# P times V in bursts of eight: batch size and copy position in an attention stage on one core

## The chip, the cores and the metric

The kernel runs on one core of a Trainium2 chip, in one launch. The metric is the device time of that launch in microseconds, the median over runs. A core has TensorE (PE; its weight loads are shown as PEld), VectorE (DVE), ScalarE (ACT), GpSimd (POOL) and SyncE (SP), which run their own instruction streams and meet only at semaphores.

## What is computed

```python
x = x + 0.5 * ffn(layernorm(x))        # x: 2048 x 128, float32
x = x + attention(layernorm(x))        # 16 heads of 8, rotary q and k, softmax over 2048 keys
x = x + 0.5 * ffn(layernorm(x))

# in attention, for each head:
scores = q @ k.T / sqrt(8)
attn = softmax(scores)
out = attn @ v
return concat(out) @ wo.T + bo

# ffn: ternary weights (128 -> 512 -> 128), exact gelu, layernorm between them
```

## The kernel before, in words

The program has three stages: the first feed-forward part with the projections, attention, and the second feed-forward part. The change lies in attention alone. There the 16 heads are 8 pairs, and the queries 4 chunks of 512. One unit `w` is one pair against one chunk: 32 of them. For a unit, TensorE, ScalarE and VectorE each walk through their own list of steps.

TensorE's list is `steps` (L1116). Step `k` of the 32 (`B_STEP`) of a unit is 128 keys of one head of the pair against 512 queries:

- `exp_mm` (L1074, matmul L1084) makes the scores, transposed, in one of three PSUM banks (`EXP`). It waits for `p_ready`, so that the exponential three steps back has left the bank. The scores already have the row's maximum subtracted: it stands in three rows of the operand `QS`.
- `max_mm` (L1058, matmul L1069) makes half of a 128 x 1024 block of scores for a later unit (23 blocks ahead), from which VectorE takes a maximum per query (L689). Two slots of two PSUM banks each hold these blocks (`A0`, a slot freed by `a_free`). The two matmuls of a step use different halves of the array's rows.
- After every fourth step (`BATCH = 4`), `pv_batch` (L1087, matmul L1095) multiplies the four exponentials of the batch before with V. They are float32, and each of the four goes to its own 32 columns of the array and 32 partitions of one PSUM bank (`PO`): two heads, even and odd key tiles. The sums grow in `PO` over the unit.
- After step 23 (`SPLIT - 1`) comes `shared` (L1099): the maxima of the next unit are transposed, and the finished sums of the unit before are turned and added by four small matmuls (L1112).
- In the last pass, `late` (L1134) slips transposes and the output projection of the finished chunks in behind some steps (`LATE`, L81).

ScalarE's list is `exps` (L897): `exp_unit` (L883, L887) turns a bank of scores into a slot of `ring`, which has 16 slots of 128 x 512 float32; every `BATCH` of them it waits (L886) until the batch that used these slots has been multiplied. After exponential `OUT_AT` (4) of a unit, `take_out` (L890, L895) copies the finished sums of the unit before from `PO` to `outT`; the first `pv_batch` of the unit waits for that copy (`po_free`, L1090).

The order of TensorE's work is thus written out by hand: a burst of P times V stands between the matmuls of one step and those of the next, and all of them are executed in order. SyncE and GpSimd only load query operands and rows of maxima, one unit or more ahead. The first three of the four chunks are a hardware loop (`Fori`), the last one is straight code, and its last units have no `max_mm` left.

A float32 matmul leaves two records in the trace: L1095 has 2048 records for 1024 multiplications, and the burst of four is x8.

Of the kernel before, what the change touches and what calls it, by code (L numbers as in the profile page):

```python
# [42 lines left out]

A_STEP = 2 * CT * 2
B_STEP = 2 * NT
BATCH = 4
NB = B_STEP // BATCH
LEAD = 23
PRING = 16
# [3 lines left out]
SHARED_AT = 12  # L53
SPLIT = 2 * SHARED_AT
TOP_AT = 2 * A_STEP - LEAD
OUT_AT = 4

A_IT = PAIRS * A_STEP
B_IT = PAIRS * B_STEP
# [9 lines left out]
def shared_slot(w, last=False):  # L69

    units = LEAD + A_STEP * w + SHARED_AT
    return (min(units, A_IT) if last else units) + w + 1
# [8 lines left out]
LATE = {(6, 5): ("T", 0), (6, 6): ("O", 0), (6, 7): ("T", 1), (7, 0): ("O", 1), (7, 1): ("F", 0),  # L81
        (7, 2): ("T", 2), (7, 3): ("O", 2), (7, 5): ("F", 1), (7, 7): ("F", 2)}
# [13 lines left out]
C_ONE = 1  # L96
C_RING = PRING // BATCH

# [11 lines left out]
def macaron(nc, x, wq, bq, wk, bk, wv, bv, wo, bo, w_fc, ln_w, ln_b, w_proj, out):  # L110
    rope_dram = nc.inline_tensor(rope_tables(), name="rope_tables").ap()

    with ExitStack() as ctx:
        def sb(name, shape, dt=F32):
            return ctx.enter_context(nc.sbuf_tensor(name, shape, dt))
# [22 lines left out]
        ring = sb("ring", [P, PRING, CS])  # L138
# [121 lines left out]
        def late_banks(c):  # L260

            return (PR[1] + 1, PR[1]) if c == NC - 1 else (A0 + 1, A0 + 3)
# [547 lines left out]
        def _(act):  # L810
# [72 lines left out]
            def exp_unit(k, c):  # L883
                act.wait_ge(b_ready, c * B_IT + k + 1)
                if k % BATCH == 0:
                    act.wait_ge(pv_done, c * PV_IT + k // BATCH + 1)  # L886
                a.activation(ring[:, k % PRING, :], ps[:, EXP[k % C_EXP], :], ACT.Exp, scale=SCALE)\  # L887
                    .then_inc(p_ready, 1)

            def take_out(i, c):  # L890

                act.wait_ge(pv_done, c * PV_IT + (i + 1) * NB + C_RING)

                act.wait_ge(a_ready, c * SLOT_IT + shared_slot(i - 1, type(c) is int) + 1)
                a.copy(outT[:, i % 2, :], ps[:, PO, :]).then_inc(po_free, 1)  # L895

            def exps(w, start, stop, c):  # L897
                for k in range(start, stop):
                    exp_unit(w * B_STEP + k, c)
                    if k == OUT_AT and (w or type(c) is not int):  # L900
                        take_out(w - 1, c)
# [16 lines left out]
        def _(pe):  # L918
# [30 lines left out]
            for n in range(2):  # L949
                for k in range(KH):  # L950
                    last = t.transpose(psb[:, TR[n], k * P:(k + 1) * P], tern[:, n, k * P:(k + 1) * P], identb[:, :])
# [106 lines left out]
            def max_mm(m, c):  # L1058

                n, x = m // 2, m % 2  # L1060
                i, u, s = n // A_STEP, n % A_STEP, unit_slot(n)
                j = i % PAIRS
                h, q, half = u % 2, u // 2 % CT, u // (2 * CT)
                if x == 0:
                    if u == 0:
                        pe.wait_ge(q_in[j], (c + i // PAIRS + 1) * 16)
                    slot_free(s, c)
                rows = slice(HR * h, HR * h + R_QK)
                mm = t.matmul(ps[:, A0 + 2 * (s % 2) + x, :], QS[rows, j, q * P:(q + 1) * P],  # L1069
                              KT[rows, j, (2 * half + x) * 512:(2 * half + x + 1) * 512], start=True, stop=True)  # L1070
                if x:
                    mm.then_inc(a_ready, 1)

            def exp_mm(i, k, c):  # L1074

                b, r4 = k // BATCH, k % BATCH
                h, kt = r4 // 2, 2 * b + r4 % 2
                n, j = i * B_STEP + k, i % PAIRS
                if k == 0:
                    pe.wait_ge(m_in[j], (c + i // PAIRS + 1) * 32)  # L1080

                pe.wait_ge(p_ready, c * B_IT + n + (C_EXP if n == SPLIT else 1))
                rows = slice(HR * h, HR * h + R_ALL)
                t.matmul(ps[:, EXP[n % C_EXP], :], KT[rows, j, kt * P:(kt + 1) * P], QS[rows, j, :],  # L1084
                         start=True, stop=True).then_inc(b_ready, 1)

            def pv_batch(i, b, c):  # L1087

                if b == 0:
                    pe.wait_ge(po_free, c * PAIRS + i + C_ONE)  # L1090
                pe.wait_ge(p_ready, c * B_IT + i * B_STEP + (b + 1) * BATCH + C_EXP)
                for r4 in range(BATCH):
                    h, kt = r4 // 2, 2 * b + r4 % 2
                    col = (2 * (i % PAIRS) + h) * VW
                    mm = t.matmul(ps[32 * r4:32 * r4 + 32, PO, :], Vx[:, kt, col:col + 32],  # L1095
                                  ring[:, (b * BATCH + r4) % PRING, :], start=(b == 0), stop=(b == NB - 1))
                mm.then_inc(pv_done, 1)

            def shared(w, c, last=False):  # L1099


                s = shared_slot(w, last)
                if not last or w < PAIRS - 1:
                    pe.wait_ge(mp_ready, c * PAIRS + w + 2)
                slot_free(s, c)
                if not last or w < PAIRS - 1:
                    mm = t.transpose(psb[0:2 * 3 * CT, A0 + 2 * (s % 2) + 1, 0:P], mp[:, (w + 1) % 2, :],
                                     identb[:, :])
                if type(c) is not int or w > 0 or last:
                    pe.wait_ge(po_free, c * PAIRS + w + C_ONE)  # L1110
                    for q in range(CT):
                        mm = t.matmul(ps[:, A0 + 2 * (s % 2), q * 2 * VW:(q + 1) * 2 * VW],  # L1112
                                      outT[:, (w - 1) % 2, q * P:(q + 1) * P], pick[:, :], start=True, stop=True)
                mm.then_inc(a_ready, 1)

            def steps(w, start, stop, c, last=False):  # L1116

                for k in range(start, stop):
                    exp_mm(w, k, c)
                    m = w * B_STEP + k + 2 * LEAD  # L1120
                    if not last or m < 2 * A_IT:
                        max_mm(m, c)
                    if k % BATCH == BATCH - 1:
                        b = k // BATCH
                        if b:
                            pv_batch(w, b - 1, c)
                        elif w or type(c) is not int:
                            pv_batch(w - 1, NB - 1, c)
                    if k == SPLIT - 1:
                        shared(w, c, last)  # L1130
                    if last and k % BATCH == BATCH - 1 and (w, k // BATCH) in LATE:
                        late(*LATE[w, k // BATCH])

            def late(kind, c):  # L1134

                if kind == "O":
                    pe.wait_ge(taken, TURNED["T", c] + 1)
                    pe.wait_ge(x1_ready, c + NC + C_TWO)
                    for i in range(CT):
                        last = t.matmul(ps[:, late_banks(c)[1], i * D:(i + 1) * D], XOT[:, i * P:(i + 1) * P],  # L1140
                                        WT[:, 3, :], start=True, stop=True)
                    last.then_inc(o_ready, 1)
                    return
                if kind == "T":
                    pe.wait_ge(xo_ready, c + 1)
                else:
                    pe.wait_ge(xn_ready, c + 2 * NC + 1)
                if TURNED[kind, c]:
                    pe.wait_ge(taken, TURNED[kind, c])
                else:  # L1150

                    pe.wait_ge(a_free, (NC - 1) * SLOT_IT + shared_slot(PAIRS - 2, True) + 1)
                for i in range(CT):
                    last = t.transpose(ps[:, late_banks(c)[0], i * P:(i + 1) * P], (XO if kind == "T" else xn)[:, i, :],
                                       ident[:, :])
                last.then_inc(turned, 1)
# [10 lines left out]
            for m in range(2 * (TURNS - 2), 2 * LEAD):  # L1167
# [5 lines left out]
                if m == 2 * (LEAD - A_STEP) + SPLIT - 1:  # L1173
                    shared(-1, 0)
            pe.wait_ge(xt_ready, 2 * NC + C_ONE)
            steps(0, 0, SPLIT, 0)
            with pe.Fori(0, NC - 1) as c:
                steps(0, SPLIT, B_STEP, c)
                for w in range(1, PAIRS):
                    steps(w, 0, B_STEP, c)  # L1180
                steps(PAIRS, 0, SPLIT, c)
            steps(0, SPLIT, B_STEP, NC - 1, True)
            for w in range(1, PAIRS):
                steps(w, 0, B_STEP, NC - 1, True)
            pv_batch(PAIRS - 1, NB - 1, NC - 1)
            shared(PAIRS, NC - 1, True)

# [42 lines left out]
```

## Time and profile before

| | |
|---|---|
| median of 3 runs | 894.6 us (891.29 to 894.69) |
| the profiled execution | 889.24 us |
| its span, first to last instruction | 887.4 us |
| mean granted TensorE clock | 0.953 of full speed |
| attention stage, first exponential to the last P times V | 151.6 to about 836.5 us |
| exponentials (L887) | 1024, mean 605 ns |
| maxima (L689) | 512, mean 1219 ns |

A row of a timeline has the start in us, the length in us from the first start to the last end, the engine, the line and operation, what it writes and reads with shapes, how many instructions are merged in it, and in brackets the idle time of the engine before them with what released it. Instructions of one engine can overlap, so several in one row are shorter than their sum. A row of windows has, for each engine, busy time and instructions, and PEclk, the granted clock as a share of full speed.

### The profile page before, as it was taken

How to read it: one execution, taken by the hardware profiler on the slowest of the kernel's cores; microseconds unless marked ns; L12 is line 12 of the kernel's file. 1: busy time of each engine (PE TensorE's matmuls, PEld its weight loads, DVE VectorE, ACT ScalarE, POOL GpSimd, SP SyncE). 2: the span in 40 equal slices, each digit the busy share in tenths (PEclk: the TensorE clock that was granted, in tenths of full speed). 3: DMA queues.
4: the chain of work that ended last, by engine and by line, in shares of the span. 5: the costliest groups of instructions: out<-in, count | busy, mean ns of one | idle time of the engine just before them, and what ended most of it. 6: DMA issues, size and time to landing. Idle time of an engine off the chain costs nothing.

```text
span 887.4 us, 16511 instructions
## 1 busy us (share of the span) xinstructions
PE 794.1 (89%) x5207; PEld 271.5 (31%) x5207; DVE 772.9 (87%) x1043; ACT 606.2 (68%) x1144; POOL 112.1 (13%) x273
## 2 busy tenths in 40 slices
PE   5876679999999998999999899999999999998885
PEld 3654431222222222222222222222222222223364
DVE  6889988899999997999999889999999999984376
ACT  2214751788888886888778778888888888884611
POOL 3344330000000000001000000000000000001023
PEclk9997885999999998999999999999999999998999
DMA  4000010000000000000000000000000000000001
GB/s 101 1 1 0 0 48 1 7 7 8 8 7 8 8 8 9 8 7 7 8 7 7 10 8 7 7 8 13 8 8 1 1 2 1 2 1 1 1 12 36
DMA packets 8239, 8.72 MB, mean 10 GB/s; under 512 B 2784, under 2 KB 6496, under 8 KB 8160
## 3 DMA queue, kind: packets, MB, share of 16 engines
q0 software_dynamic: 1536, 4.20, 1.3%
q1 hardware_dynamic: 4272, 2.82, 1.1%
q10 hardware_dynamic: 2352, 0.66, 0.4%
q8 instruction: 48, 0.79, 0.4%
q14 instruction: 31, 0.25, 0.1%
HBM read 2.23 MB, written 1.05 MB: 4 GB/s over the span
## 4 chain that ended last, share of the span: by engine, by line
PE 57%; ACT 17%; issue 13%; DVE 8%; POOL 3%; ACTq 1%; DVEq 0%; DMA 0%; POOLq 0%; SPq 0%
PE ps L1095 25%; PE ps L1084 21%; ACT ring L887 15%; PE ps L1069 4%; PE ps L1112 4%; ACT outT L895 2%; DVE mh L689 2%; POOL XB L341 1%; PE ps L942 1%; DVE xn L461 1%; DVE X L647 1%; DVE terms L642 1%; DVE ring L637 1%; PE ps L1140 1%; ACTq L886 1%
## 5 line engine op out<-in xcount | busy, mean ns | idle before, releaser
L887 ACT ACTIVATE ring<-ps 128x512 f32<-128x512 f32 x1024 | 532.6, 605 | 163.8 <-PE ps L1084 162.1
L689 DVE TENSOR_REDUCE mh<-ps 128x1 f32<-128x1024 f32 x512 | 603.1, 1219 | 38.0 <-PE ps L1069 25.3
L1069 PE MATMUL ps<-KT,QS 48*128 48x512 bf16 x1024 | 354.7, 396 | 3.4 <-DVE mh L689 2.5
L1084 PE MATMUL ps<-QS,KT 51*128 51x512 bf16 x1024 | 314.9, 390 | 33.0 <-ACT ring L887 20.6
L1095 PE MATMUL ps<-ring,Vx 128*32 128x512 f32 x2048 | 276.7, 613 | 2.6
L1084 PEld LDWEIGHTS ps<-QS,KT 51*128 51x128 bf16 x1024 | 76.1, 94 | 334.3 <-ACT ring L887 294.3
L1069 PEld LDWEIGHTS ps<-KT,QS 48*128 48x128 bf16 x1024 | 75.6, 94 | 84.0 <-DVE mh L689 60.1
L409 POOL TENSOR_TENSOR mp<-zeros,top 128x8 bf16<-128x8 f32 x32 | 6.2, 194 | 470.1 <-DVE top L699 470.1
L1095 PEld LDWEIGHTS ps<-ring,Vx 128*32 128x32 f32 x2048 | 40.6, 108 | 64.6 <-issue 49.9
L829 ACT ACTIVATE ring<-ps 128x512 f32<-128x512 f32 x32 | 17.2, 602 | 45.7 <-DVE ring L524 25.3
L418 POOL DMA_DIRECT2D QS<-QT x32 | 18.1, 567 | 154.3 <-PE ps L1084 154.3
L1038 PE MATMUL ps<-identb,terms 128*128 128x128 bf16 x256 | 22.9, 256 | 14.0 <-ACT QT L874 8.7
L1112 PE MATMUL ps<-pick,outT 128*128 128x18 f32 x256 | 34.1, 267 | 0.8 <-ACT outT L895 0.8
L990 PE MATMUL ps<-WpC,ring 128*128 128x129 f32 x256 | 31.3, 281 | 3.2 <-ACT ring L829 2.4
L1112 PEld LDWEIGHTS ps<-pick,outT 128*128 128x128 f32 x256 | 31.0, 191 | 10.1 <-issue 10.1
L990 PEld LDWEIGHTS ps<-WpC,ring 128*128 128x128 f32 x256 | 30.8, 197 | 5.5 <-issue 3.0
L931 PE MATMUL ps<-QT,WfcT 128*128 128x512 f32 x64 | 29.5, 601 | 0.8 <-ACT QT L825 0.7
L519 DVE TENSOR_TENSOR ring<-ring 128x512 f32<-128x512 f32 x32 | 22.7, 714 | 7.7 <-ACT ring L829 7.7
L1038 PEld LDWEIGHTS ps<-identb,terms 128*128 128x128 bf16 x256 | 18.6, 115 | 20.6 <-ACT QT L874 11.2
L708 DVE COPY mrow<-ps 24x128 bf16<-24x128 bf16 x32 | 6.8, 211 | 20.3 <-PE ps L1112 20.3
L524 DVE TENSOR_TENSOR ring<-ring 128x512 f32<-128x512 f32 x24 | 21.2, 884 | 1.8
L461 DVE TENSOR_SCALAR xn<-X,mv,rs 128x128 f32<-128x128 f32 (+1 forms) x48 | 21.4, 532 | 0.9 <-PE ps L926 0.5
(110 smaller groups left out, 385.9 us busy)
## 6 DMA issues: line engine op xcount, KB each, us to landing
QS<-QT POOLq DMA_DIRECT2D x32, 128.0 KB, 2.0
QS<-mrow SPq DMA_DIRECT2D x64, 3.0 KB
out_dram<-X SPq DMA_DIRECT2D x4, 256.0 KB, 2.3
wfc_n<-in_L_ffn_W_fc_dram SPq DMA_DIRECT2D x1, 256.0 KB, 3.1
wpj_n<-in_L_ffn_W_proj_dram SPq DMA_DIRECT2D x1, 256.0 KB, 3.6
rope<-rope_tables ACTq DMA_DIRECT2D x1, 128.0 KB, 6.2
w_n<-in_L_attn_wq_dram ACTq DMA_DIRECT2D x1, 64.0 KB, 3.4
w_n<-in_L_attn_wk_dram ACTq DMA_DIRECT2D x1, 64.0 KB, 6.6
```

Source lines behind the costliest of these rows:

```text
L461: last = v.tensor_scalar(xn[:, i, :], rows_of(src, c, i), mv[:, b * CT + i, 0:1], rs[:, b * CT + i:b * CT + i + 1], ALU.subtract, ALU.mult)
L519: v.tensor_tensor(sq[:, k, :], hid[:, k, :], hid[:, k, :], ALU.mult)
L524: return v.tensor_tensor(sqsum[:, k - 1, :], sqsum[:, k - 2, :] if k > 1 else sq[:, 0, :], sq[:, k, :], ALU.add)
L689: v.tensor_reduce(mh[:, n // A_STEP % 2, at:at + 1], ps[:, slot_banks(s), :].rearrange("p a b -> p (a b)"), AX.X, ALU.max).then_inc(a_free, 1)
L887: a.activation(ring[:, k % PRING, :], ps[:, EXP[k % C_EXP], :], ACT.Exp, scale=SCALE)\
L931: t.matmul(ps[:, FC + k, :], WfcT[:, k * P:(k + 1) * P], XF[:, bass.ds(c * CS, CS)], start=True, stop=True).then_inc(fc_ready, 1)
L990: last = t.matmul(out_tile(i, parity)[:, 0:D + 1], hid[:, k, i * P:(i + 1) * P], WpC[:, k, :], start=(k == 0), stop=(k == KH - 1))
L1038: last = t.transpose(psb[:, TR[m % 3], (j * CT + i) * P:(j * CT + i + 1) * P], terms[:, n, i, 4 * e + 2 * j:4 * e + 2 * j + 2, :] .rearran ...
L1069: mm = t.matmul(ps[:, A0 + 2 * (s % 2) + x, :], QS[rows, j, q * P:(q + 1) * P], KT[rows, j, (2 * half + x) * 512:(2 * half + x + 1) * 512] ...
L1084: t.matmul(ps[:, EXP[n % C_EXP], :], KT[rows, j, kt * P:(kt + 1) * P], QS[rows, j, :], start=True, stop=True).then_inc(b_ready, 1)
L1095: mm = t.matmul(ps[32 * r4:32 * r4 + 32, PO, :], Vx[:, kt, col:col + 32], ring[:, (b * BATCH + r4) % PRING, :], start=(b == 0), stop=(b == ...
L1112: mm = t.matmul(ps[:, A0 + 2 * (s % 2), q * 2 * VW:(q + 1) * 2 * VW], outT[:, (w - 1) % 2, q * P:(q + 1) * P], pick[:, :], start=True, sto ...
```

## The change

The batch is eight exponentials: `NB` falls from 8 to 4 batches per unit, `C_RING` (`PRING // BATCH`, L97) from 4 to 2, so the ring of 16 holds two batches. `pv_batch` runs after every eighth step, and multiplies the eight exponentials of the batch before in one go; a new constant `GROUP = 4` keeps the mapping of a step to head, key tile and 32-column group as it was. ScalarE waits for the ring once in eight. `OUT_AT` goes from 4 to 8: the copy of the finished sums stands behind exponential 8 of the next unit. The late work of the last pass keeps its steps.

```diff
--- before.py
+++ after.py
@@ -43,7 +43,8 @@
 
 A_STEP = 2 * CT * 2
 B_STEP = 2 * NT
-BATCH = 4
+GROUP = 4
+BATCH = 8
 NB = B_STEP // BATCH
 LEAD = 23
 PRING = 16
@@ -53,7 +54,7 @@
 SHARED_AT = 12
 SPLIT = 2 * SHARED_AT
 TOP_AT = 2 * A_STEP - LEAD
-OUT_AT = 4
+OUT_AT = 8
 
 A_IT = PAIRS * A_STEP
 B_IT = PAIRS * B_STEP
@@ -1073,8 +1074,8 @@
 
             def exp_mm(i, k, c):
 
-                b, r4 = k // BATCH, k % BATCH
-                h, kt = r4 // 2, 2 * b + r4 % 2
+                r4 = k % GROUP
+                h, kt = r4 // 2, 2 * (k // GROUP) + r4 % 2
                 n, j = i * B_STEP + k, i % PAIRS
                 if k == 0:
                     pe.wait_ge(m_in[j], (c + i // PAIRS + 1) * 32)
@@ -1089,11 +1090,12 @@
                 if b == 0:
                     pe.wait_ge(po_free, c * PAIRS + i + C_ONE)
                 pe.wait_ge(p_ready, c * B_IT + i * B_STEP + (b + 1) * BATCH + C_EXP)
-                for r4 in range(BATCH):
-                    h, kt = r4 // 2, 2 * b + r4 % 2
+                for k in range(b * BATCH, (b + 1) * BATCH):
+                    r4 = k % GROUP
+                    h, kt = r4 // 2, 2 * (k // GROUP) + r4 % 2
                     col = (2 * (i % PAIRS) + h) * VW
                     mm = t.matmul(ps[32 * r4:32 * r4 + 32, PO, :], Vx[:, kt, col:col + 32],
-                                  ring[:, (b * BATCH + r4) % PRING, :], start=(b == 0), stop=(b == NB - 1))
+                                  ring[:, k % PRING, :], start=(k < GROUP), stop=(k >= B_STEP - GROUP))
                 mm.then_inc(pv_done, 1)
 
             def shared(w, c, last=False):
@@ -1128,8 +1130,8 @@
                             pv_batch(w - 1, NB - 1, c)
                     if k == SPLIT - 1:
                         shared(w, c, last)
-                    if last and k % BATCH == BATCH - 1 and (w, k // BATCH) in LATE:
-                        late(*LATE[w, k // BATCH])
+                    if last and k % GROUP == GROUP - 1 and (w, k // GROUP) in LATE:
+                        late(*LATE[w, k // GROUP])
 
             def late(kind, c):
```

## Rows read from the trace of the kernel before

**Rows 1.** The page: busy time by engine, the exponentials, and the chain by engine.

```profile
PE 794.1 (89%) x5207; PEld 271.5 (31%) x5207; DVE 772.9 (87%) x1043; ACT 606.2 (68%) x1144; POOL 112.1 (13%) x273
...
L887 ACT ACTIVATE ring<-ps 128x512 f32<-128x512 f32 x1024 | 532.6, 605 | 163.8 <-PE ps L1084 162.1
...
PE 57%; ACT 17%; issue 13%; DVE 8%; POOL 3%; ACTq 1%; DVEq 0%; DMA 0%; POOLq 0%; SPq 0%
```

**Rows 2.** Windows: busy time of each engine, granted clock (PEclk), by stretch.

```profile
23.00:71.00 48.00, 36.97 (x209) 27.36 (x210) 42.01 (x107) 8.54 (x16) 21.06 (x21) 0.93 0.00 1
...
172.00:332.00 160.00, 152.07 (x1053) 41.26 (x1045) 148.92 (x153) 130.71 (x255) 11.46 (x43) 1.00 0.03 8
```

**Rows 3.** Timeline of ScalarE, loop code.

```profile
301.52 0.58 ACT L895 COPY outT<-ps 128x512 f32<-128x512 f32 x1
...
308.52 2.06 ACT L887 ACTIVATE ring<-ps 128x512 f32<-128x512 f32 x4 [0.41 <-PE ps L1084]
...
310.99 2.06 ACT L887 ACTIVATE ring<-ps 128x512 f32<-128x512 f32 x4 [0.41 <-PE ps L1084]
...
314.50 2.06 ACT L887 ACTIVATE ring<-ps 128x512 f32<-128x512 f32 x4 [1.44 <-PE ps L1084]
...
322.41 0.58 ACT L895 COPY outT<-ps 128x512 f32<-128x512 f32 x1
...
322.87 3.73 ACT L887 ACTIVATE ring<-ps 128x512 f32<-128x512 f32 x7
```

**Rows 4.** Timeline of TensorE, one period of the loop.

```profile
309.18 0.39 PE L1084 MATMUL ps<-QS,KT 51*128 51x512 bf16 x1
...
309.50 1.06 PE L1095 MATMUL ps<-ring,Vx 128*32 128x512 f32 x8
...
310.49 0.39 PE L1084 MATMUL ps<-QS,KT 51*128 51x512 bf16 x1
...
310.94 0.38 PE L1084 MATMUL ps<-QS,KT 51*128 51x512 bf16 x1
...
311.11 0.39 PE L1069 MATMUL ps<-KT,QS 48*128 48x512 bf16 x1
...
311.65 0.39 PE L1084 MATMUL ps<-QS,KT 51*128 51x512 bf16 x1 [0.15 <-ACT ring L887]
```

**Rows 5.** Timelines of TensorE: first and second round of a burst; dense float32 matmuls.

```profile
302.16 0.64 PE L1095 MATMUL ps<-ring,Vx 128*32 128x512 f32 x4
...
302.61 0.61 PE L1095 MATMUL ps<-ring,Vx 128*32 128x512 f32 x4
...
840.46 1.88 PE L931 MATMUL ps<-QT,WfcT 128*128 128x512 f32 x4
```

**Rows 6.** Timeline of VectorE, loop code.

```profile
303.83 7.22 DVE L689 TENSOR_REDUCE mh<-ps 128x1 f32<-128x1024 f32 x6 [0.27 <-PE ps L1069]
...
314.71 9.73 DVE L689 TENSOR_REDUCE mh<-ps 128x1 f32<-128x1024 f32 x8
```

**Rows 7.** Timeline of ScalarE, last pass (between two copies: one unit).

```profile
706.21 0.58 ACT L895 COPY outT<-ps 128x512 f32<-128x512 f32 x1
...
726.55 0.58 ACT L895 COPY outT<-ps 128x512 f32<-128x512 f32 x1
```

**Rows 8.** Timeline of ScalarE where no maxima are left.

```profile
817.82 2.06 ACT L887 ACTIVATE ring<-ps 128x512 f32<-128x512 f32 x4 [0.58 <-PE ps L1084]
...
820.79 2.06 ACT L887 ACTIVATE ring<-ps 128x512 f32<-128x512 f32 x4 [0.91 <-PE ps L1084]
...
824.27 2.06 ACT L887 ACTIVATE ring<-ps 128x512 f32<-128x512 f32 x4 [1.41 <-PE ps L1084]
...
826.66 2.06 ACT L887 ACTIVATE ring<-ps 128x512 f32<-128x512 f32 x4 [0.33 <-PE ps L1084]
```

**Rows 9.** Timeline of ScalarE behind the stall between two passes.

```profile
338.10 2.06 ACT L887 ACTIVATE ring<-ps 128x512 f32<-128x512 f32 x4 [4.15 <-PE ps L1084]
...
341.89 2.06 ACT L887 ACTIVATE ring<-ps 128x512 f32<-128x512 f32 x4 [1.73 <-PE ps L1084]
```

## The prediction

> **What bounds the kernel now.** I read the page first: TensorE, VectorE and ScalarE are all busy for most of the span, and the chain that ended last runs over TensorE for 57% and ScalarE for 17% [rows 1]. So no single engine's busy time is the answer. The windows show the same through the attention stage (from 151.64 to 836 us; 1024 exponentials): in 160 us TensorE is busy for 152.07, VectorE for 148.92, ScalarE for 130.71, at full clock [rows 2]. Everything that the change touches lies in this stage, and it repeats, so I read it as a rhythm.
>
> The rhythm on ScalarE: four exponentials in 2.06 us, then an idle stretch of 0.41 us that ends with the matmul at L1084; starts at 308.52 and 310.99, so four exponentials per 2.47 us [rows 3]. Four alone would take less: (2.06 - 0.605)/3 = 0.485 us from start to start (0.605 us is the mean of one [rows 1]), 1.94 us for four. ScalarE is held up once in four, always at the exponential behind a burst of P times V. One period is a closed loop [rows 4, 5]: the score matmul of the last step of a four starts at 309.18, when a PSUM bank of the three comes free; the burst starts 0.32 later (309.50) and takes 0.99 until the next score matmul can start (310.49); its exponential starts 0.50 later (310.99) and takes 0.61; its end frees the bank for the next such score matmul, 0.05 later (311.65). Sum 0.32 + 0.99 + 0.50 + 0.61 + 0.05 = 2.47. The other three exponentials run beside the burst.
>
> Does VectorE set this period too? Its maxima follow each other every (9.73 - 1.22)/7 = 1.22 us at most, (7.22 - 1.22)/5 = 1.20 at best, so it needs 2.40 to 2.43 of each 2.47 us [rows 6]: close, not above. The decisive rows come from the end of the stage, in the last pass, where no maxima are left: the period is 826.66 - 824.27 = 2.39 us [rows 8]. Earlier in that pass, with all the maxima, a unit of 32 exponentials lasts 726.55 - 706.21 = 20.34 us [rows 7]; taking 1.04 us for its shared step (below), 19.3 are left for eight periods: 2.41. So maxima or none, the period is the same (the pass is straight code; that it is 0.08 shorter than in the loop I put down to wait arithmetic on ScalarE). The loop of TensorE and ScalarE sets the time, and the burst is on it. An extra batch of transposes behind a burst gave 820.79 - 817.82 = 2.97, which is 2.39 plus its own length [rows 8]. In [rows 3] the shared transposes and four small matmuls give 314.50 - 310.99 = 3.51, 1.04 more than 2.47. What is put behind a burst is paid in full.
>
> In the loop a unit lasts 322.41 - 301.52 = 20.89 us (between two copies of finished sums): 8 x 2.47 + 1.04 = 20.80, so the copy itself costs 0.09 [rows 3]. There are 32 units, 24 of them by loop code.
>
> **The change, step by step.** Take eight exponentials as the new period and count from the start of the score matmul of step 7 of the eight, which waits as before for the fourth exponential back to free its bank.
> 1. The burst. It starts at 0.32 as now. In a burst of four, each multiplication leaves two records; the four run side by side, and the second round starts 302.61 - 302.16 = 0.45 us behind the first [rows 5]. Two rounds are 0.90, the whole takes 0.99. I take 0.90 for the added four: 1.89 in all. Bounds: 0.99 each if nothing is shared between the fours; 2 x (1.88 - 0.60)/3 = 0.85 if the second four runs as densely as the records of L931 do [rows 5]. The score matmul of step 8 starts at 0.32 + 1.89 = 2.21, its exponential 0.50 later at 2.71. The exponential that freed the bank began 0.05 + 0.61 before zero, so the third behind it ends at 3 x 0.485 + 0.605 - 0.66 = 1.40, and ScalarE idles 1.31 us, where it idled 0.41 (by the same count 1.81 - 1.40).
> The 0.09 that is left over in today's burst, and 0.32 - 0.22 = 0.10 before it (score matmuls otherwise follow each other at (310.94 - 310.49)/2 = 0.22 [rows 4]), look like a price of going in and out of the 32-column form. The Trainium skill, TensorEngine Tiling, section Key Properties, says that a change of tiling mode, unlike a change of tile, drains TensorE. The trace agrees in that both ends of a burst have such gaps. By that rule the added four costs 0.90, without it 0.99, which is 128 x 0.09 = 12 us more.
> 2. The half without a burst. Exponentials 8 to 12 then follow without a hole: 12 starts at 2.71 + 4 x 0.485 = 4.65, ends at 5.26, and the next score matmul of a step 7 starts at 5.31. Against 2 x 2.47 = 4.94 now. So the second half gives back 2.47 - 1.94 = 0.53, and the burst takes 0.90: 0.37 net.
> 3. VectorE. TensorE starts no maxima for 2.2 us. The first unit of scores after the burst is ready at 2.21 + 0.22 + 0.39 + 0.05 = 2.87; VectorE, which needs 4.8 us per eight, has by then run dry and starts it at once; two maxima later, at 2.87 + 1.20 + 1.22 = 5.29, the slot is free that the block of step 14 needs, and the score matmul of step 15 is queued behind it: 5.35 instead of 5.31. Today both slots hold work for VectorE during a burst (8 maxima without a hole [rows 6]); this cover is gone. I take 5.35 (in the last pass the ScalarE way gives 5.23, and VectorE's 5.35 decides). Bounds: nothing, if the wait doesn't fall in with the score matmul, to 0.2 more per period, about one stall as it stands at L1069 now (its matmul starts at 311.11, its partner at 310.94 [rows 4]).
> 4. The copy of the sums, later. Now it lies behind exponential 4, in the hole before 8: of its 0.46 us (322.87 - 322.41 [rows 3]), 0.09 show. After the change it stands behind exponential 8, and there is no hole until 12, which frees the bank on which the next period hangs. ScalarE's way becomes 5.31 + 0.46 = 5.77 in that period: 0.42 over 5.35, 0.33 more than its price now. Bounds 0 and 0.46. Its readers are far: TensorE wants the bank at step 15, the shared matmuls at step 23.
> 5. The shared step sits at step 23, behind a burst now and then: 1.04 in both. Semaphores: half as many batch increments and waits, on no path that I find; the ring wait of exponential 8 is for the burst that its own score matmul is behind anyhow. No DMA is moved; the queues of SyncE and GpSimd lead by many steps.
> 6. The end: the last batch waits for the last exponential and is eight: +0.9 us by step 1. Two or three of the late transposes of the last pass now fall outside a burst, where TensorE has time: -2 us.
>
> Sum. A unit in the loop: 4 x 5.35 + 1.04 + 0.42 = 22.86, minus 20.89 = 1.97; 24 units: 47 us. The last pass: 22.86 - 20.34 = 2.52; 8 units: 20 us. The end: -1. Together +66 us. The profiled execution took 889.24 us (span 887.4), so 955; the median of the runs is 894.6, 5.4 above it, and my number is for the median: 894.6 + 66 = **960 us**.
>
> **Rivals.**
> a) VectorE holds TensorE harder: each maximum after the burst waits, and the score matmul queued behind it too, so the losses of ScalarE and VectorE add up. For: VectorE has hardly more than 0.04 to 0.07 of 2.47 us to spare. Against: with the longer period it gets 0.5 us. Price 0.25 more per eight, 128 x 0.25 = 32: 992 us. Chance 0.10.
> b) The clock falls. TensorE is granted full clock (2.4 GHz) through the stage, except behind stalls such as the one of 4.15 us on ScalarE before 338.10; behind it, at half clock (1.2 GHz) at first, the period of four is 341.89 - 338.10 = 3.79 us, 1.32 more [rows 9]. The change lowers TensorE's work per time by some 7%. Against: from 23 to 71 us the granted clock was 0.93 with TensorE busy 36.97 of 48 us, though no less a share than I expect here [rows 2]. If the stage were granted that 0.93, 0.14 of the periods would be at half clock, each longer by those 1.32 and another 0.9 for the added four: 128 x 0.14 x 2.2 = 40 us: 1000 us. Chance 0.05.
> c) VectorE is the real bound, and TensorE's absence hides behind its two slots: 895 us, no change. For: it is busy 149 of 160 us. Against: the period without maxima is the same [rows 7, 8]. Chance 0.04.
> d) Faster: TensorE is the bound (busy 152 of 160 us), and half of the entries and exits of bursts are saved, 128 x (0.10 + 0.09) = 24 us: 871 us. It decides only if the burst never leaves ScalarE dry, that is if a burst is shorter than the exponentials that stand ready behind it: 0.32 + 1.89 + 0.50 must be under the 1.40 of step 1, and even today's 1.81 is not. This is what the rule of TensorEngine Tiling in the Trainium skill would give if it stood alone. Chance 0.03.
> That the change doesn't do what it says: the eight stand in one loop without a wait between them, so no split is possible; I give it 0.01, at 895 us.
>
> **How the numbers follow.** The forecast has 0.77, a) 0.10, b) 0.05, c) 0.04, d) 0.03, no effect 0.01. Bounds of the terms: burst -6 to +12 us, VectorE -8 to +26, copy -13 to +2. All at their ends give 66 - 27 = 39 and 66 + 40 = 106: 934 to 1001; for the spread of the runs (891.29 to 894.69) two more below. The range 932 to 1000 holds the forecast and a), and just reaches b); c), d) and no effect stay out with 0.08. A measurement of this kernel can tell about 0.5% (4.5 us) from no change. Faster: 0.03; same: 0.05; slower: 0.92.
>
> **What would show it.** In the profile after: ScalarE's row x8, or two rows with one hole in eight of about 1.3 us before it, released by L1084; eight exponentials per 5.35 us; sixteen records of L1095 in about 1.95 us, the next score matmul 1.89 behind the first; a unit of about 22.9 us; a VectorE that waits about 0.5 us per eight for L1069. Step 1 is wrong if the burst is not 1.85 to 2.0; step 3 if the period differs from 5.35 with a burst of 1.89; step 4 if the period with the copy is no 0.4 longer than the others. The prediction as a whole is wrong if ScalarE's hole stays at 0.4, or if the granted clock leaves 1.0 in the steady stretches.

## The result, and the profile after

The changed kernel takes 1095.9 us (median of 4 runs, 1088.8 to 1098.6) against 892.9 us for the kernel before beside it (4 runs, 890.4 to 894.7): 1.226 times as long, 95% interval 1.219 to 1.233. The direction was forecast, the size was not: 960 us was predicted, with 932 to 1000 as the range. The runs of a kernel spread, by 2% in one case below, and every ratio here goes by those within 1.5% of the fastest.

The page of the profile after: the span, busy times, the line of granted clock by slice, and the three engines' main groups.

```profile
span 1096.8 us, 16358 instructions
...
PE 965.2 (88%) x5206; PEld 311.5 (28%) x5207; DVE 767.9 (70%) x1043; ACT 594.5 (54%) x1144; POOL 112.1 (10%) x273
...
PEclk9978657888897878788978887889788987887899
...
L690 DVE TENSOR_REDUCE mh<-ps 128x1 f32<-128x1024 f32 x512 | 599.9, 1218 | 182.9 <-PE ps L1070 181.7
...
L888 ACT ACTIVATE ring<-ps 128x512 f32<-128x512 f32 x1024 | 520.4, 629 | 379.9 <-PE ps L1085 379.5
...
L1097 PE MATMUL ps<-ring,Vx 128*32 128x512 f32 x2048 | 356.1, 831 | 0.0
```

Two of these lines as the page before has them:

```profile
PEclk9997885999999998999999999999999999998999
...
L1095 PE MATMUL ps<-ring,Vx 128*32 128x512 f32 x2048 | 276.7, 613 | 2.6
```

The work is the same, the instructions nearly so [rows 1]: VectorE's maxima have the same mean, 1218 ns against 1219. But P times V now has 831 ns per record where the page before had 613, and the PEclk line, which stood at 9 in the middle but for one slice of 8, is mostly at 7 and 8 through the attention stage, with single slices of 9. ScalarE idles 379.9 us in front of its exponentials, 163.8 before.

Windows of the changed kernel in the attention stage (columns as in [rows 2]; the third number from the end is the granted clock). The first stretch lies in the first pass of the loop in every kernel here:

```profile
172.00:332.00 160.00, 145.56 (x801) 39.02 (x805) 113.61 (x118) 98.05 (x196) 9.36 (x36) 0.83 0.02 6
...
355.00:500.00 145.00, 131.95 (x713) 35.22 (x709) 99.87 (x104) 86.65 (x173) 7.79 (x30) 0.81 0.02 6
```

Granted clock 0.83 and 0.81; the kernel before has 1.00 in both stretches. The first timeline is ScalarE's. A row x8 is one period; the number in brackets is the hole behind a burst.

```profile
405.99 4.03 ACT L888 ACTIVATE ring<-ps 128x512 f32<-128x512 f32 x8 [3.80 <-PE ps L1085]
...
413.28 0.60 ACT L888 ACTIVATE ring<-ps 128x512 f32<-128x512 f32 x1 [3.26 <-PE ps L1085]
...
413.77 0.58 ACT L896 COPY outT<-ps 128x512 f32<-128x512 f32 x1
...
414.24 3.56 ACT L888 ACTIVATE ring<-ps 128x512 f32<-128x512 f32 x7
...
420.64 4.03 ACT L888 ACTIVATE ring<-ps 128x512 f32<-128x512 f32 x8 [2.85 <-PE ps L1085]
...
427.15 4.03 ACT L888 ACTIVATE ring<-ps 128x512 f32<-128x512 f32 x8 [2.48 <-PE ps L1085]
...
434.32 4.03 ACT L888 ACTIVATE ring<-ps 128x512 f32<-128x512 f32 x8 [3.14 <-PE ps L1085]
...
439.79 0.60 ACT L888 ACTIVATE ring<-ps 128x512 f32<-128x512 f32 x1 [1.45 <-PE ps L1085]
```

There are two kinds of period, those at full clock (2.4 GHz) and those that are partly at half clock (1.2 GHz). From 434.32 to 439.79 one lasts 5.47 us: that is the schedule at full clock, 0.12 over the forecast 5.35. From 405.99 to 413.28 one lasts 7.29, and its hole is 3.26 us instead of 1.45. (From 427.15 to 434.32 are 7.17 us.) TensorE's timeline shows the difference, first a burst at half clock, then one at full clock with the thin half of the period ahead of it. Between them stands the end of another thin half and its burst:

```profile
409.27 3.48 PE L1097 MATMUL ps<-ring,Vx 128*32 128x512 f32 x16
...
412.69 0.47 PE L1085 MATMUL ps<-QS,KT 51*128 51x512 bf16 x1
...
415.89 0.39 PE L1085 MATMUL ps<-QS,KT 51*128 51x512 bf16 x1
...
416.38 0.61 PE L1085 MATMUL ps<-QS,KT 51*128 51x512 bf16 x1
...
416.92 3.29 PE L1097 MATMUL ps<-ring,Vx 128*32 128x512 f32 x16
...
420.14 0.39 PE L1085 MATMUL ps<-QS,KT 51*128 51x512 bf16 x1
...
433.81 0.39 PE L1085 MATMUL ps<-QS,KT 51*128 51x512 bf16 x1
...
436.90 0.39 PE L1070 MATMUL ps<-KT,QS 48*128 48x512 bf16 x1
...
436.99 0.38 PE L1085 MATMUL ps<-QS,KT 51*128 51x512 bf16 x1
...
437.13 0.38 PE L1070 MATMUL ps<-KT,QS 48*128 48x512 bf16 x1
...
437.43 1.92 PE L1097 MATMUL ps<-ring,Vx 128*32 128x512 f32 x16
...
439.29 0.39 PE L1085 MATMUL ps<-QS,KT 51*128 51x512 bf16 x1
```

At full clock the next score matmul starts 1.86 us behind the start of the burst, at half clock 3.42. Between bursts, over 3.6 us (433.81 to 437.43), TensorE has eight pairs of score matmuls, which follow each other 0.22 us apart where nothing holds them, and otherwise it waits. The rows show where the clock changes: a score matmul takes 0.39 at 415.89 and 0.61 at 416.38, the last one before the burst, the burst behind it takes 3.29, and the score matmul at 420.14 takes 0.39 again. So here the clock falls at the end of a thin half, and is back after the burst. Through the stage the falls show in the second half of such a stretch or in the burst behind it, the ends of a pass aside. In TensorE's timeline from 170 us on, 60 of 123 bursts take over 2.7 us and 63 under 2 us.

Of the 203 us, how much is schedule and how much is clock? That is what the experiments are about. The ratio of each is to the kernel before, run on the same chip.

### The profile page after: what moved, and what is told of

Same layout as the page of the kernel before. It is cut to its first block, busy times and chain, and to the rows that moved or that the text cites. A ratio compares the mean times of both kernels' runs of the same rounds, so it can differ in the third digit from the quotient of the medians.

```text
span 1096.8 us, 16358 instructions
## 1 busy us (share of the span) xinstructions
PE 965.2 (88%) x5206; PEld 311.5 (28%) x5207; DVE 767.9 (70%) x1043; ACT 594.5 (54%) x1144; POOL 112.1 (10%) x273
## 3 DMA queue, kind: packets, MB, share of 16 engines
q1 hardware_dynamic: 4272, 2.82, 0.9%
## 4 chain that ended last, share of the span: by engine, by line
PE 59%; DVE 16%; issue 13%; ACT 9%; DVEq 1%; POOL 1%; ACTq 0%; DMA 0%; POOLq 0%; SPq 0%
PE ps L1097 32%; PE ps L1085 11%; DVE mh L690 10%; PE ps L1070 9%; ACT ring L888 7%; PE ps L1114 3%; ACT outT L896 2%; PE ps L932 1%; DVE xn L462 1%; DVEq L524 1%; PE ps L943 1%; POOL XB L342 1%; PE ps L1027 1%; DVE X L648 0%; DVE terms L643 0%
## 5 line engine op out<-in xcount | busy, mean ns | idle before, releaser
L690 DVE TENSOR_REDUCE mh<-ps 128x1 f32<-128x1024 f32 x512 | 599.9, 1218 | 182.9 <-PE ps L1070 181.7
L888 ACT ACTIVATE ring<-ps 128x512 f32<-128x512 f32 x1024 | 520.4, 629 | 379.9 <-PE ps L1085 379.5
L1085 PE MATMUL ps<-QS,KT 51*128 51x512 bf16 x1024 | 381.6, 423 | 60.8 <-ACT ring L888 43.3
L1070 PE MATMUL ps<-KT,QS 48*128 48x512 bf16 x1024 | 368.0, 435 | 18.1 <-DVE mh L690 11.7
L1097 PE MATMUL ps<-ring,Vx 128*32 128x512 f32 x2048 | 356.1, 831 | 0.0
L1085 PEld LDWEIGHTS ps<-QS,KT 51*128 51x128 bf16 x1024 | 88.0, 96 | 341.7 <-ACT ring L888 241.6
L1097 PEld LDWEIGHTS ps<-ring,Vx 128*32 128x32 f32 x2048 | 65.8, 134 | 180.1 <-issue 133.3
L1070 PEld LDWEIGHTS ps<-KT,QS 48*128 48x128 bf16 x1024 | 84.7, 97 | 111.1 <-DVE mh L690 74.5
L830 ACT ACTIVATE ring<-ps 128x512 f32<-128x512 f32 x32 | 17.2, 602 | 44.3 <-DVE ring L525 25.5
L1027 PE MATMUL ps<-WT,ring 128*128 128x384 f32 x32 | 19.0, 765 | 5.5 <-ACT ring L826 5.5
```

The source lines that it names most:

```text
L690: v.tensor_reduce(mh[:, n // A_STEP % 2, at:at + 1], ps[:, slot_banks(s), :].rearrange("p a b -> p (a b)"), AX.X, ALU.max).then_inc(a_free, 1)
L1027: t.matmul(ps[:, FC + i, 0:3 * D], XT[:, i * P:(i + 1) * P], WT[:, 0:3, :].rearrange("p n d -> p (n d)"), start=True, stop=True).then_inc( ...
```

## The experiments

**Bursts of four in the changed kernel.** The eight of a batch are multiplied as four behind step 3 and four behind step 7. All else of the change stays: the ring wait once in eight, one semaphore step per batch, the copy behind exponential 8.

```diff
...
-                    if k % BATCH == BATCH - 1:
-                        b = k // BATCH
+                    if k % GROUP == GROUP - 1:
+                        b, half = k // BATCH, k % BATCH // GROUP
                         if b:
-                            pv_batch(w, b - 1, c)
+                            pv_batch(w, b - 1, c, half)
...
```

> The changed kernel, but the eight of a batch are multiplied as four behind step 3 and four behind step 7; ring wait once in eight and the copy behind exponential 8 stay. If the burst length alone makes the loss (stall behind a burst of 1.86 us, and the lower granted clock that comes with it): 890 to 900 us, granted clock about 0.95, eight exponentials per 4.94 us as before. If the coarser ring wait or the later copy carries a good part of the loss: over 920 us.

Measured: 888.9 us, ratio 0.995 (0.993 to 0.998), granted clock 0.942. ScalarE's timeline:

```profile
405.12 2.07 ACT L888 ACTIVATE ring<-ps 128x512 f32<-128x512 f32 x4 [1.44 <-PE ps L1085]
...
407.51 2.06 ACT L888 ACTIVATE ring<-ps 128x512 f32<-128x512 f32 x4 [0.33 <-PE ps L1085]
...
409.98 2.06 ACT L888 ACTIVATE ring<-ps 128x512 f32<-128x512 f32 x4 [0.41 <-PE ps L1085]
...
412.38 2.06 ACT L888 ACTIVATE ring<-ps 128x512 f32<-128x512 f32 x4 [0.33 <-PE ps L1085]
```

The whole loss is gone, so it hangs on the length of the burst (and of the thin half that comes with it), and not on the coarser waits or the later copy by themselves. The result is even 0.5% faster than the kernel before: in the loop the periods of four alternate between 2.39 (405.12 to 407.51) and 2.47 us (407.51 to 409.98), where the kernel before had 2.47 throughout [rows 3]. That fits the ring wait, which now stands ahead of every second four only: in these rows the four after a hole of 0.41 us (409.98) has it, the ones after 0.33 don't. No run moves this wait by itself. It is the fastest version of this study.

**A fuller thin half.** The score matmul is issued twice in steps 2 to 6 of each eight, into the same bank with the same values. The burst, and all waits, stay as in the changed kernel.

```diff
+DOUBLED = (2, 3, 4, 5, 6)
...
-                t.matmul(ps[:, EXP[n % C_EXP], :], KT[rows, j, kt * P:(kt + 1) * P], QS[rows, j, :],
-                         start=True, stop=True).then_inc(b_ready, 1)
+                for _ in range(1 + (k % BATCH in DOUBLED)):
+                    mm = t.matmul(ps[:, EXP[n % C_EXP], :], KT[rows, j, kt * P:(kt + 1) * P], QS[rows, j, :],
+                                  start=True, stop=True)
+                mm.then_inc(b_ready, 1)
```

> The changed kernel with the score matmul issued twice in steps 2 to 6 of each eight (same values into the same bank), so that TensorE works in the half without a burst too: more work, same burst. Theory (the clock is granted by how evenly TensorE is busy, and half of the loss or more is the clock): clock over 0.93 and 945 to 975 us, faster than the changed kernel by 12%. Rival (the clock falls because of the long burst of 32-column matmuls itself, or the loss is all schedule): clock stays near 0.82, time 1095 to 1140 us.

Measured: 978.4 us, ratio 1.094 (1.086 to 1.102), granted clock 0.939. TensorE does more, and the kernel is 117 us faster than the changed one. First a window, then ScalarE's timeline:

```profile
172.00:332.00 160.00, 154.66 (x1076) 46.34 (x1080) 132.29 (x138) 114.83 (x230) 10.94 (x42) 1.00 0.02 7
```

```profile
404.40 0.58 ACT L897 COPY outT<-ps 128x512 f32<-128x512 f32 x1
...
409.69 4.03 ACT L889 ACTIVATE ring<-ps 128x512 f32<-128x512 f32 x8 [1.26 <-PE ps L1087]
...
416.22 4.03 ACT L889 ACTIVATE ring<-ps 128x512 f32<-128x512 f32 x8 [2.50 <-PE ps L1087]
...
421.73 4.03 ACT L889 ACTIVATE ring<-ps 128x512 f32<-128x512 f32 x8 [1.48 <-PE ps L1087]
...
427.22 0.60 ACT L889 ACTIVATE ring<-ps 128x512 f32<-128x512 f32 x1 [1.47 <-PE ps L1087]
...
427.72 0.58 ACT L897 COPY outT<-ps 128x512 f32<-128x512 f32 x1
```

The clock is 1.00 (in 355 to 500 us it is 0.96; of that, 360 to 380 us, with the stall between two passes of the loop, has 0.74, and every other 20 us have 1.00), and the periods are those that the changed kernel had at full clock: 427.22 - 421.73 = 5.49 us, 5.51 between 416.22 and 421.73, hole 1.48. So at most 978.4 - 893 = 85 us are the schedule's, and some 117 are the clock's (1095.9 - 978.4). The units agree: one lasts 427.72 - 404.40 = 23.32 us in the loop against 20.89 before, and 804.03 - 780.87 = 23.16 in the last pass against 20.34, 24 x 2.43 + 8 x 2.82 = 81 us. The burst is as long as in the changed kernel, so it isn't the long burst as such that lowers the clock: 4 of 127 bursts take over 2.7 us.

**Three added matmuls, in two places.** The same edit with `DOUBLED = (3, 4, 5)`, the middle of the thin half, and with `DOUBLED = (7, 0, 1)`, on both sides of the burst.

> As e2_fill, but only three score matmuls in eight are issued twice, in the middle of the thin half (steps 3, 4, 5). Theory (the clock falls because TensorE's work is thin for 3.6 us at a time): the middle of the thin half is what counts, clock over 0.90, time 960 to 1000 us. Rival (a threshold of total work): the same clock as e6_near3, whatever it is.

> The same three added matmuls per eight, put next to the burst (steps 7, 0, 1), where TensorE is dense anyway; the thin half stays as thin as in the changed kernel. Theory: clock stays under 0.87, time over 1070 us (two of the three also lengthen the hole, 0.44 us per eight). Rival (total work): the same clock as e5_fill3.

Measured: 992.8 us (ratio 1.111, 1.104 to 1.117) in the middle, and 1159.1 us (1.299, 1.294 to 1.305) beside the burst. The windows, first of the one in the middle, then of the one beside the burst:

```profile
172.00:332.00 160.00, 147.53 (x999) 42.82 (x999) 129.24 (x135) 111.55 (x223) 10.93 (x42) 0.98 0.02 7
...
355.00:500.00 145.00, 132.62 (x877) 38.76 (x878) 112.81 (x119) 97.86 (x195) 9.35 (x36) 0.95 0.02 7
```

```profile
172.00:332.00 160.00, 144.88 (x829) 41.09 (x833) 108.61 (x113) 95.99 (x188) 9.43 (x36) 0.86 0.02 6
...
355.00:500.00 145.00, 130.35 (x739) 37.37 (x733) 95.04 (x100) 84.24 (x163) 7.66 (x30) 0.84 0.02 6
```

The same added work keeps the clock at 0.98 and 0.95 in one place and leaves it at 0.86 and 0.84 in the other; 13 of 127 bursts take over 2.7 us in the one, 54 of 116 in the other. The second window of both holds a stall between two passes, so the first is the better to compare. The sum of the work per eight exponentials doesn't decide, its place does. (Beside the burst the matmuls also lengthen the period, to 424.59 - 418.60 = 5.99 us at full clock, 0.51 more: 128 x 0.51 = 65 us, and this kernel is 63 us slower than the changed one at a slightly higher clock.) That it is the thinnest stretch that decides is the reading that fits, not a thing these runs separate from others.

**Bursts of four at the pace of the changed kernel.** To the kernel before, two small copies on ScalarE are added in each four exponentials, so that its period is as long as half of the changed kernel's, while TensorE's work stays evenly spread.

```diff
...
+                if k % BATCH == 1:
+                    act.wait_ge(spared, c * PV_IT + k // BATCH)
+                    a.copy(spare[:, 0:H], warm_in[:, :])
+                    a.copy(spare[:, H:H + PACE], warm_in[:, 0:PACE]).then_inc(spared, 1)
```

> The kernel before, bursts of four, with two small copies added on ScalarE in each four exponentials, so that its period goes from 2.47 to about 2.75 us: TensorE then works at the same mean rate as the changed kernel at full clock (eight exponentials per 5.5 us), but evenly. If the mean share of work decides the clock: granted clock near 0.82 and over 1040 us. If it is the bunching (1.9 us of burst, then 3.6 us of thin work): clock stays at 0.95 and time is 890 + 256 x 0.28 = 960 us.

Measured: 975.3 us, ratio 1.093 (1.089 to 1.097), granted clock 0.950. A window, then three periods in ScalarE's timeline:

```profile
172.00:332.00 160.00, 145.91 (x933) 39.83 (x933) 132.27 (x135) 155.70 (x336) 10.38 (x39) 1.00 0.02 7
```

```profile
402.07 2.23 ACT L890 ACTIVATE ring<-ps 128x512 f32<-128x512 f32 x4
...
404.80 2.27 ACT L890 ACTIVATE ring<-ps 128x512 f32<-128x512 f32 x4
...
407.54 2.30 ACT L890 ACTIVATE ring<-ps 128x512 f32<-128x512 f32 x4
```

The period is 2.74 us for four, 5.48 for eight, as in the changed kernel at full clock, and the granted clock is 1.00. TensorE is busy for 145.91 of 160 us. The changed kernel's 145.56 hold records at half clock, which last longer, so the busy times say little; what is the same is the work per 5.48 us. By 0.22 us for a pair of score matmuls and the lengths of the bursts it is (2 x 0.99 + 8 x 0.22)/5.48 = 0.68 here, (1.86 + 1.76)/5.48 = 0.66 in the changed kernel at full clock, and (1.86 + 11 x 0.22)/5.99 = 0.71 with three matmuls beside the burst, an estimate from these rows. The clocks are 1.00, 0.83 and 0.86: the mean doesn't decide. At the same mean rate four and four keep the clock, and eight don't. The 15 us over the expected 960 I put down to ScalarE: busy for 155.70 of 160 us, it has no hole left for the copy of the sums, and a unit lasts 23.40 us (copies at 397.56 and 420.96), 0.44 more than 8 x 2.74 + 1.04. An exponential and the copy follow each other 0.46 us apart, so 32 x 0.44 = 14 us can be the copies'.

**VectorE taken off.** The kernel with the fuller thin half, with each maximum over 256 of its 1024 columns; three quarters of the scores are left out of it. The exponentials take a hundredth of their scale.

```diff
...
                 v.tensor_reduce(mh[:, n // A_STEP % 2, at:at + 1],
-                                ps[:, slot_banks(s), :].rearrange("p a b -> p (a b)"),
+                                ps[:, A0 + 2 * (s % 2) + 1, 0:256],
...
-                a.activation(ring[:, k % PRING, :], ps[:, EXP[k % C_EXP], :], ACT.Exp, scale=SCALE)\
+                a.activation(ring[:, k % PRING, :], ps[:, EXP[k % C_EXP], :], ACT.Exp, scale=0.01 * SCALE)\
```

> e2_fill with VectorE's maxima over 256 of the 1024 columns, so that VectorE never holds TensorE (it leaves out three quarters of each maximum; the exponentials take a smaller scale so that they stay finite). My step 3: without VectorE the plain period at full clock is the ScalarE way, 5.31 us instead of the 5.50 of e2_fill, the one with the copy stays at 5.78; a unit is 0.5 to 0.6 us shorter, 978 - 18 = 960 us. Rival (VectorE costs nothing at full clock, the period is set by the burst and ScalarE): within 4 us of 978.

Measured: 950.0 us (4 runs, 934.2 to 954.1), ratio 1.055 (1.043 to 1.067), 28 us less than with whole maxima by the medians. ScalarE's timeline:

```profile
400.94 4.03 ACT L889 ACTIVATE ring<-ps 128x512 f32<-128x512 f32 x8 [2.30 <-PE ps L1087]
...
406.23 4.03 ACT L889 ACTIVATE ring<-ps 128x512 f32<-128x512 f32 x8 [1.26 <-PE ps L1087]
...
411.52 0.60 ACT L889 ACTIVATE ring<-ps 128x512 f32<-128x512 f32 x1 [1.26 <-PE ps L1087]
...
412.01 0.58 ACT L897 COPY outT<-ps 128x512 f32<-128x512 f32 x1
...
417.30 4.03 ACT L889 ACTIVATE ring<-ps 128x512 f32<-128x512 f32 x8 [1.26 <-PE ps L1087]
...
434.69 0.58 ACT L897 COPY outT<-ps 128x512 f32<-128x512 f32 x1
```

The plain period is 406.23 - 400.94 = 5.29 us, 5.31 by the forecast's count without VectorE, and the period with the copy is 417.30 - 411.52 = 5.78. A unit lasts 22.68 us (412.01 to 434.69) where it lasted 23.32 (404.40 to 427.72). VectorE costs 0.2 us in each plain period and in the one with the shared step (6.32 us, 423.62 - 417.30, against 6.53), and nothing in the one with the copy (5.78 in both). Over 32 units the 0.64 us are 20 us. The other 8 are not accounted for; the runs of this kernel spread by 20 us.

**The copy of the sums one exponential earlier.** `OUT_AT = 7`, first in the changed kernel, then in the one with the fuller thin half.

> The changed kernel with the copy behind exponential 7, in ScalarE's hole. My step 4 (the copy lies open behind exponential 8; the trace at full clock shows 5.78 against 5.48 us for that period): 31 x 0.30 = 9 us less, about 1086 us. Rival (the hole is set elsewhere, by VectorE or the clock): within 4 us of 1096.

> e2_fill (clock held) with the copy of the sums behind exponential 7, in ScalarE's hole. My step 4: the period with the copy falls from 5.78 to the plain 5.50 us, 31 x 0.28 = 9 us, 978 to about 969 us. Rival (the copy then waits for the whole burst of which it takes the sums, and exponential 8 behind it): the gain is under 3 us, since the copy can't start before the burst ends, 2.2 us after the score matmul of step 7, and the exponential is due at 2.7.

Measured: 1087.8 us in the changed kernel (ratio 1.220, 1.214 to 1.225; its own was 1.219 to 1.233, so the intervals overlap), and 979.0 us with the fuller half (1.095, 1.091 to 1.100), against 978.4: nothing. ScalarE's timeline of the latter:

```profile
402.52 0.59 ACT L897 COPY outT<-ps 128x512 f32<-128x512 f32 x1 [1.18 <-PE ps L1100]
...
403.01 4.03 ACT L889 ACTIVATE ring<-ps 128x512 f32<-128x512 f32 x8
...
408.51 4.03 ACT L889 ACTIVATE ring<-ps 128x512 f32<-128x512 f32 x8 [1.47 <-PE ps L1087]
...
425.75 0.59 ACT L897 COPY outT<-ps 128x512 f32<-128x512 f32 x1 [1.18 <-PE ps L1100]
```

The copy sits in the hole, but it starts only when the burst has ended (its releaser is the P times V line), as the rival of the expectation had it, and exponential 8 behind it starts late. What the one period gains the other loses: the unit is 23.23 us, 23.32 before. The 8 us of the first run are not explained by the schedule; the granted clock there may depend on it (0.812 against 0.816 in the profiled executions, so not plainly), and I leave them open.

## Why the prediction was wrong

The direction and the mechanism on ScalarE were right, the size was wrong by a factor of three (203 us for 66). The step that failed is the clock: the sum took every period at full clock and put a fall at nothing, leaving it to rival b) with a chance of 0.05 and 40 us. The runs showed 117 us for it. With the clock held the change gives 978.4 us, inside the range.

**The clock.** Rival b)'s argument against a fall was a stretch early in the kernel with a low busy share at a granted clock of 0.93 (busy 36.97 of 48 us, a share of 0.77), and the estimate that TensorE's work per time falls by 7% only. The forecast called 0.77 no less a share than it expected in this stage; by the same records 0.95 x 0.93 = 0.88 was to be expected. Both arguments compare means. The runs show that the mean is not what counts: the paced kernel has the same mean rate and keeps 1.00; three matmuls per eight restore 0.98 in the middle of the thin half, and leave 0.86 beside the burst. The trace of before held the numbers to ask the right question: within 2.47 us it has a burst of 0.99, so no stretch without dense work was longer than 1.5 us; I had worked out that this grows to 3.5 and didn't look at it as a pattern for the clock. The price per period was about right: 7.29 or 7.17 us against 5.47 is 1.7 to 1.8 us in the timeline above, 2.2 was taken, and 117 us over the 60 slow bursts are 1.95. What was far too low is how many: 0.14 of the periods in the forecast, 60 of 123 bursts in the trace. The Trainium skill, TensorE: Matmul & The Clock Gate, section Why this matters for your kernels, wants TensorE kept busy and warns of idle gaps between bursts. The trace agrees in that the clock falls at the end of the stretch between two bursts; but no wait of a score matmul there is longer than 0.6 us, so work with short waits in it was too thin as well.

**Step 1, the burst.** Forecast 1.89 us, measured 1.86 at full clock, nearer to the bound of 1.84 (0.99 + 0.85) than I took. The added four cost 0.87, not the 0.99 of a burst of its own, which is in line with the rule on drains that I cited, though no run takes the change of form apart from the rest. The hole of 1.31 is 1.45 in the trace.

**Step 2, the half without a burst.** Right: eight exponentials in 4.03 us without a hole, 0.49 apart; without VectorE the period is 5.29 against 5.31.

**Step 3, VectorE.** Right in its mechanism, too small in its size. The first unit is ready 0.68 behind the first score matmul (from 433.81 to 434.49, where VectorE starts; 0.66 in the forecast) and the maximum's matmul of step 14 starts at 436.90, 3.09 behind it (forecast 5.34 - 2.21 = 3.13). But I let the burst follow 0.32 behind step 15's score matmul. The matmul for the maxima of step 15 starts 0.23 behind that of step 14, at 437.13, and the burst stands behind both, at 437.43, 0.44 behind step 15's score matmul (436.99). The period becomes 5.48 instead of 5.35. Of this VectorE's share is 5.50 - 5.29 = 0.21 us; I had 0.04, with 0.2 as the bound. By the units of the run without it this comes to 20 us.

**Step 4, the copy.** The period with it is 5.78, and 5.77 was forecast. Its price is 0.28 over the plain period, not 0.42, since VectorE has lengthened the plain one. That an earlier copy would save this, as I expected in two of the runs, is wrong: behind exponential 7 it costs the same.

**Steps 5 and 6.** The shared step cost 1.02 us with the clock held (416.22 - 409.69 = 6.53 less 5.51); coarser waits cost nothing, as the kernel with bursts of four and waits of eight shows. The -1 us of step 6 was not looked at.

**The sum.** At held clock the change costs up to 978.4 - 893 = 85 us where I had 66, and the unit shows why: 5.50 + 5.51 + 5.78 + 6.53 = 23.32 us, 22.86 forecast, and nearly all of the 0.46 is VectorE's in three of the four periods. The rest of 203 us is the clock. Rival a), 0.25 us more per eight for VectorE, was not met in full: 0.17 more, in three periods of four. Rivals c) and d) fell: VectorE and TensorE are busy most of the time, yet neither hid the burst, and no saving at the ends of a burst could show.

## What to carry to other kernels

Before making a burst longer, ask two things: who runs dry beside it (count the ready work of the consumer, here three banks, against the burst's length), and how thin the stretch between bursts becomes for the granted clock. A mean busy share answers neither; spread dense work evenly, and where TensorE has idle time in a thin stretch, even repeated matmuls there can pay (117 us here, against the changed kernel; the kernel before is still 85 us faster). The coarser waits that a bigger batch gives can be had without the bigger burst.

## What was not expected of the hardware

The granted clock fell to 0.81 in a stretch where TensorE's records, longer at half clock, cover 91% of the time (131.95 of 145 us) and no wait of it for ScalarE's exponentials in front of L1085 is longer than 0.6 us; and five added matmuls per eight exponentials made the kernel 117 us faster. Which measure of TensorE's work decides was not found out: these runs only show that the place of the work counts and not its sum. Whether VectorE's hold on TensorE has a part in the fall is open: the run with short maxima has the added matmuls too, and their clock of 1.00 is there with whole maxima as well.
